# Expert tiles of 128 rows, and TensorE alternating between the next tile's first product and this tile's second

## The reference, cut to what matters

```python
x = x + xattn(layernorm(x), ctx_768, ...)             # (4, 512, 256)
n = layernorm(x)
probs = softmax(n @ Wr.T); top_v, top_i = top_k(probs, 2); top_v /= sum(top_v)
for e in range(8):
    w_e = sum(where(top_i == e, top_v, 0))
    h = gelu(n @ W1[e].T + b1[e])                     # 256 -> 1024
    out += (h @ W2[e].T + b2[e]) * w_e                # 1024 -> 256
x = x + out
```

## Time and profile before

| | before |
|---|---|
| median of 3 runs (lowest, highest) | 484.67 us (478.1, 484.67) |
| the profiled execution's own time | 480.82 us |
| its span, first to last instruction | 478.9 us |
| TensorE busy | 411.0 us, 86% |
| VectorE, ScalarE, GpSimd busy | 319.3, 198.8, 142.2 us |
| mean granted TensorE clock | 0.944 |

### The profile page before, as it was taken

The page is one execution under the profiler, slowest core; times in us unless marked ns, Lnnn a source line. Parts: engine busy times, 40 slices in busy tenths (PEclk is TensorE's granted clock), DMA queues, the critical chain, the costliest instruction groups (busy, mean ns, idle before and its releaser), DMA issues.

```text
span 478.9 us, 9857 instructions
## 1 busy us (share of the span) xinstructions
PE 411.0 (86%) x2876; PEld 317.9 (66%) x2877; DVE 319.3 (67%) x895; ACT 198.8 (42%) x339; POOL 142.2 (30%) x133
## 2 busy tenths in 40 slices
PE   3989899779898654039999999999999999999991
PEld 1345547436465543028888888888888888888880
DVE  2104755876769575917777777777777777777771
ACT  0214956775667464203443343333333434343330
POOL 8200300304253446800333222222223333222222
PEclk9999999999989975559999999999999999999997
DMA  7930037227534715240233332222222233332211
GB/s 241 327 117 0 22 117 247 90 88 237 203 121 130 258 65 167 78 144 1 46 50 67 53 53 44 46 44 44 44 44 44 44 49 62 56 54 44 44 22 23
DMA packets 32482, 43.46 MB, mean 91 GB/s; under 512 B 3088, under 2 KB 27920, under 8 KB 32336
## 3 DMA queue, kind: packets, MB, share of 16 engines
q1 hardware_dynamic: 19840, 27.24, 19.5%
q0 software_dynamic: 8880, 12.69, 13.8%
q10 hardware_dynamic: 3744, 3.31, 2.0%
HBM read 28.45 MB, written 14.78 MB: 90 GB/s over the span
## 4 chain that ended last, share of the span: by engine, by line
PE 73%; DVE 11%; ACT 4%; issue 4%; DMA 4%; POOL 2%; SPq 1%; POOLq 1%; DVEq 0%; ACTq 0%
PE o_ps L653 25%; PE s_ps L633 12%; PE t_ps L633 12%; PE proj L473 5%; PE s_ps L507 4%; PE o_ps L526 4%; PE proj L621 3%; PE proj L465 3%; DVE w2l L953 2%; PE proj L494 2%; POOL rows L404 2%; DMA xt<-rows 2%; PE proj L481 2%; PE t_ps L517 1%; DMA w2l<-ctxT 1%
## 5 line engine op out<-in xcount | busy, mean ns | idle before, releaser
L436 POOL DMA_INDIRECT out<-y,idx x46 | 72.5, 1576 | 196.7 <-DVE y L1189 189.7
L826 ACT ACTIVATE g<-s_ps,b_sb,down 128x256 f32<-128x256 f32 x92 | 46.9, 560 | 157.1 <-PE s_ps L633 157.1
L653 PE MATMUL o_ps<-w2h,gl 128*128 x368 | 100.3, 273 | 0.0
L653 PE MATMUL o_ps<-w2h,gh 128*128 x368 | 100.3, 273 | 0.0
L653 PE MATMUL o_ps<-w2l,gh 128*128 x368 | 100.3, 273 | 0.0
L1157 DVE TENSOR_SCALAR gh<-g,up 128x512 f16<-128x512 f32 x92 | 44.8, 486 | 40.9 <-ACT g L826 40.1
L1159 DVE SCALAR_TENSOR_TENSOR gl<-g,up,gh 128x512 f16<-128x512 f32 x92 | 69.1, 751 | 3.3
L826 ACT ACTIVATE g<-t_ps,b_sb,down 128x256 f32<-128x256 f32 x92 | 46.9, 559 | 13.5 <-PE t_ps L633 13.5
L404 POOL DMA_INDIRECT rows<-send,place x32 | 39.1, 1222 | 34.2 <-DVE place L1010 25.6
L653 PEld LDWEIGHTS o_ps<-w2l,gh 128*128 128x128 f16 x368 | 36.0, 98 | 4.2
L653 PEld LDWEIGHTS o_ps<-w2h,gl 128*128 128x128 f16 x368 | 36.0, 98 | 4.2
(11 more groups left out here) (160 smaller groups left out, 681.8 us busy)
## 6 DMA issues: line engine op xcount, KB each, us to landing
staged<-W1T SPq DMA_DIRECT2D x8, 1024.0 KB
staged<-W2T SPq DMA_DIRECT2D x8, 1024.0 KB
xt<-rows SPq DMA_DIRECT2D x23, 260.0 KB, 2.7
rows<-send POOLq DMA_DIRECT2D x8, 260.0 KB, 8.2
out<-x_sb ACTq DMA_DIRECT2D x4, 512.0 KB
w2l<-ctxT SPq DMA_DIRECT2D x4, 256.0 KB
x_sb<-x SPq DMA_DIRECT2D x2, 512.0 KB, 10.6
x_sb<-x ACTq DMA_DIRECT2D x2, 512.0 KB, 5.3
```

What stands on the lines that cost most here:

```text
L436: pool.indirect_dma_start(out=out, out_offset=bass.IndirectOffsetOnAxis(ap=idx[:, u, r:r + 1], axis=0), in_=y2[:, u, r, :], in_offset=None ...
L653: i = nc.tensor.matmul(y_ps[r][:, 0:D], l[:, m, r * P:(r + 1) * P], w[:, bass.ds(e, 1), m * D:(m + 1) * D].rearrange("p a n -> p (a n)"), ...
L826: i = nc.scalar.activation(g[:, m, :], h_ps[s][:, (m % MQ) * TR:(m % MQ + 1) * TR], ACT.Gelu, bias=b1_sb[:, bass.ds(e, 1), m:m + 1].rearra ...
```

## The change

The tile has 128 rows in place of 256, so `TILES` = (2·2048 + 8·127) // 128 = 39. There are 8 row buffers in place of 2. A matmul of the first product now has 128 moving columns, and there are still 48 of them to a tile; the second product has one half, so 24 matmuls with 256 moving columns. On TensorE `tile(t)` runs over the 8 chunks and at each gives out chunk `m` of the first product of tile t+1 and then chunk `m - LAG` of the second product of tile t (`LAG` = 2; the last two chunks of tile t fall into the next call). The transposes of tile t+2 stand after chunk 2. `xs`, `g`, `gh`, `gl`, `y1`, `y2` and the transposes' PSUM have two copies. The high half of the transposed rows is taken by ACT (`take_high`), the low half stays with DVE. DVE splits gelu's output in two pieces of 4 chunks each. Repeated rows get a gate of 0 (`fresh`) in place of another target, so the index arithmetic in `mark` goes, and the row number is kept as an integer. There is one scatter to a tile. The loops of PE, DVE and POOL are unrolled by 8, after 5 tiles written out (`HEAD`) and ahead of 2 (`TAIL` = 37).

```diff
-TR = 2 * P
+TR = P
-XR = 2
+XR = 8
+LAG = 2
+HEAD = 5
+TAIL = HEAD + XR * ((TILES - 2 - HEAD) // XR)
...
-                    sp.wait_ge(half_done, t * 2 - (2 * XR - 2))
+                    sp.wait_ge(added, t * 16 - (XR - 1) * 16)
...
+            def second(t, m, slot, e):
+                if m % MH == 0:
+                    pe.wait_ge(gs_ready, t * HALVES + (m // MH + 1))
+                for k, (l, w) in enumerate(((gh, w2h), (gh, w2l), (gl, w2h))):
+                    i = nc.tensor.matmul(y_ps[slot % 2][:, 0:D], l[:, slot % 2, m, :],
...
+            def tile(t, phase, ahead, e_before, e):
+                e_next = None
+                if ahead > 0:
+                    e_next = expert(t + 1)
+                    pe.wait_ge(xs_ready, t + 2)
                 for m in range(MC):
...
+                    if ahead > 0:
+                        hidden(t + 1, m, (phase + 1) % XR, e_next)
+                    if ahead > 1 and m == LAG:
+                        turn_tile(t + 2, (phase + 2) % XR)
+                    if m >= LAG:
+                        if m == LAG and (not isinstance(t, int) or t >= 2):
+                            pe.wait_ge(y_biased, t - 1)
+                        second(t, m - LAG, phase, e)
+                    elif not isinstance(t, int) or t:
+                        second(t - 1, m + MC - LAG, (phase - 1) % XR, e_before)
...
+            with pe.Fori(HEAD, TAIL - XR + 1, XR) as t:
+                experts = (expert(t - 1), expert(t))
+                for k in range(XR):
+                    experts = tile(t + k, (HEAD + k) % XR, 2, *experts)
...
+            def take_high(t, u):
+                act.wait_ge(turned, t + 1)
+                nc.scalar.activation(xs[:, u, :, 0, :], xT_ps[u][:, 0:DC * TR].rearrange("p (c n) -> p c n", c=DC),
+                                     ACT.Copy).then_inc(xs_high, 1)
```

More of the change, by code:

```diff
@@ L623, in turn_tile @@
                 i.then_inc(turned, 1)
-            def hidden(t, e):
-                pe.wait_ge(xs_ready, t + 1)
-                for m in range(MC):
[L629 to L664, removed]
+            def expert(t):
+                return pe.value_load(expert_of[0:1, bass.ds(t, 1)], min_val=0, max_val=E - 1)
+            def hidden(t, m, slot, e):
+                bank = h_ps[m // MQ]
+                if m % MQ == 0 and (not isinstance(t, int) or t):
+                    pe.wait_ge(g_ready, t * QUARTERS + (m // MQ + 1 - QUARTERS))
+                for k, (w, half) in enumerate(((w1h, 0), (w1h, 1), (w1l, 0))):
+                    for c in range(DC):
+                        at = c * M + m * P
+                        i = nc.tensor.matmul(bank[:, (m % MQ) * TR:(m % MQ + 1) * TR],
+                                             w[:, bass.ds(e, 1), at:at + P].rearrange("p a n -> p (a n)"),
+                                             xs[:, slot % 2, c, half, :], start=(k == 0 and c == 0),
+                                             stop=(k == 2 and c == DC - 1))
+                if m % MQ == MQ - 1:
+                    i.then_inc(h_full, 1)
@@ L666, in _ @@
             turn_tile(0, 0)
+            turn_tile(1, 1)
             pe.wait_ge(low_ready, UNITS)
[L668 to L673, removed]
+            experts = (None, expert(0))
+            pe.wait_ge(xs_ready, 1)
+            for m in range(MC):
+                hidden(0, m, 0, experts[1])
+            for t in range(HEAD):
+                experts = tile(t, t, 2, *experts)
@@ new lines, in _ @@
+            with pe.Fori(HEAD, TAIL - XR + 1, XR) as t:
+                experts = (expert(t - 1), expert(t))
+                for k in range(XR):
+                    experts = tile(t + k, (HEAD + k) % XR, 2, *experts)
+            experts = (expert(TAIL - 1), expert(TAIL))
+            for t in range(TAIL, TILES):
+                experts = tile(t, t % XR, min(2, TILES - 1 - t), *experts)
+            for m in range(MC - LAG, MC):
+                second(TILES - 1, m, (TILES - 1) % XR, experts[0])
@@ new lines, in tile @@
+            def tile(t, phase, ahead, e):
+                u = phase % 2
+                split(t, u, 1, e)
+                if ahead > 1:
+                    take_low(t + 2, u)
+                e_next = None
+                if ahead > 0:
+                    e_next = expert(t + 1)
+                    split(t + 1, 1 - u, 0, e_next)
+                mark(t, phase)
+                result(t, u, e)
+                return e_next
+            take_low(0, 0)
+            take_low(1, 1)
+            dve.wait_ge(b2_in, 16)
@@ L1211 @@
+            e = expert(0)
+            split(0, 0, 0, e)
+            for t in range(HEAD):
+                e = tile(t, t, 2, e)
+            with dve.Fori(HEAD, TAIL - XR + 1, XR) as t:
+                e = expert(t)
+                for k in range(XR):
+                    e = tile(t + k, (HEAD + k) % XR, 2, e)
+            e = expert(TAIL)
+            for t in range(TAIL, TILES):
+                e = tile(t, t % XR, min(2, TILES - 1 - t), e)
 def kernel(x, ctx_768, L0_xattn_Wq, L0_xattn_bq, L0_xattn_Wk, L0_xattn_bk, L0_xattn_Wv, L0_xattn_bv,
```

195 lines of the change are left out of this document (95 added, 100 removed).

## The result

The changed kernel takes 523.62 us, the median of 4 runs (522.23 to 528.71), and the kernel before 481.64 us (4 runs, 478.1 to 484.67). The ratio is 1.089, with a 95% interval of 1.077 to 1.102: 9% slower, 42 us. The profiled execution's own time is 524.5 us.

A forecast was written before the change was run, and what follows sets the result against it. The array's column streaming bounds the kernel before, TensorE's sequencer the changed one. 210.9 + 5.1 + 40.2 + 1 + 235.2 + 8 + 3.4 = 503.8, plus 9.0 and 1.9, gives 514.7; forecast 514 us, range 470 to 528.

The forecast's parts named there:

- TensorE's sequencer in place of the array: Second stage: register instructions need 0.74 us per chunk index, the array's matmuls 0.66, so the sequencer is the slower one.
- the array's pace: Rival: in timed runs the sequencer doesn't bind and the array sets 5.5 us a tile, 439.5 us; chance 0.15.
- narrow matmuls costing more: Rival: 128-column matmuls at 0.08 us; forecast stands, or 483 us with a quicker sequencer; chance 0.12 with other middling paces.
- The loop's fetch: Rival: TensorE's loop no longer fits, branches back wait 2.7 us for a fetch, 522 us; chance 0.08.
- the granted clock: Sign of being right: TensorE's clock stays at 1.00 from some 217 us on.
- Start: Second stage's start: fewer transposes and half width on DVE gain 0.9 us, first product of tile 0 at 210.9.
- Loop: TensorE's 32 loop tiles at 7.35 us are 235.2, and four round heads of 2 us are 8.
- Written-out tiles: Six tiles outside TensorE's loop at 6.7 us each, 40.2, with 1 us more while the clock is low.
- the eight row buffers: Row loads: the added buffers save nothing, since TensorE has no idle time waiting for them.
- End: Behind the loop: a written-out tile at 6.7 us, then the last tile's second product alone, 2.6 + 0.8 = 3.4 us.
- the DVE round trip: Result, then second split piece: 3.0 us against TensorE's 3.5, so no cost; 0.3 us late each tile would be 11.
- Behind the last matmul: After TensorE's last matmul: 9.0 us in place of 10.9, one scatter in the last tile saving 1.85 us.

The follow-up runs named there:

- static: Changed kernel with expert 0 for every tile on TensorE, so no reading of the expert's number or address work there; 454.47 us, ratio 0.952.
- before_static: Kernel before with expert 0 for every tile on TensorE, the choice of the expert left out; 479.03 us, ratio 1.004.
- static_w2l: Changed kernel with expert 0's weights for the `w2l` matmuls alone, 8 of 48 register instructions less a tile; 490.19 us, ratio 1.025.
- b2_third: Changed kernel with b2's load third on SP's queue, behind two row loads; 520.19 us, ratio 1.076.
- before_more: Kernel before with the expert read twice a tile, six register instructions in place of four per first-product chunk; 489.08 us, ratio 1.023.
- unrolled_pe: Changed kernel with the 32 tiles of TensorE's loop written out, nothing left out; 503.13 us, ratio 1.050.
- static_b2: Changed kernel with expert 0 for every tile on TensorE and b2's load third on SP's queue; 444.96 us, ratio 0.924.

## Why the prediction was right

The forecast was 514 us for the median and for the profiled execution 514.7; they came out at 523.6 and 524.5, so the loss is 42 us where some 34 were forecast. The mechanism, TensorE's sequencer in place of the array, is shown by static against before_static, and its price by static_w2l. The rivals (the array's pace, narrow matmuls costing more) are refuted by the same runs: the 0.055 us is there, and the array isn't what sets the pace in the change. The loop's fetch isn't a cost that shows in the change: 16 fetches of instructions, 0.26 MB, against 9, and a loop head is 2.5 to 2.6 us of idle array, which its three readings of an expert at 0.75 us and the branch account for. One sign named for being right failed: the granted clock didn't stay at 1.00 (see the last section).

By the terms of the sum:

- **Start.** First product at 211.48, predicted 210.9. The reading for tile 0's own body at 215.33, predicted 216.0.
- **Loop.** From the first head to the reading behind the last tile it is 497.23 - 255.09 = 242.1 us. Predicted were 235.2 + 8 = 243.2. Between the first and the last tile of a round the readings lie 7.18 to 7.49 us apart (predicted 7.35). That the sum is within 1.1 us is in small part luck: tiles of 7.25 us, as read above, would be 3 us less in 32, and the first tiles behind three of the heads took 7.6 to 8.2 us, with the clock at half for a part of them, which the prediction didn't have.
- **Written-out tiles.** The five ahead of the loop took 255.09 - 215.33 = 39.8 us; predicted were 5 x 6.7 + 1 = 34.5. The 5.3 us are the wait for b2 with what followed it: the gap of 4.55 us at 222.79, and after it matmuls at half the clock up to 227.2, where two wide ones are 0.21 us apart. Without the wait, in b2_third, the same five took 34.05. In the change the four tiles behind the wait took 6.75 to 7.19 us each. This term was left out: the prediction counted the eight row buffers as saving nothing, and didn't ask what SP's queue does with seven row loads ahead of b2.
- **End.** From 497.23 to the last matmul 13.9 us, predicted 6.7 + 3.4 = 10.1. Two more readings of the expert behind the loop are 1.3 us, and the clock falls behind them (below). Another 1.3 us is the DVE round trip that the prediction had weighed for each tile and found just hidden. In the loop it is, but in the last tile no first product stands between: VectorE forms tile 37's result and then splits the last piece, and TensorE waits for it at 509.88.
- **Behind the last matmul.** 522.5 - 511.08 = 11.4 us, predicted 9.0. The single scatter was to save 1.85 us, but it has to wait for the one before it to land. GpSimd's timeline, against the earlier trace rows:

```profile
509.36 1.82 POOL L437 DMA_INDIRECT out<-y,xt  x1 [3.84 <-DVE y L1223]
514.44 1.56 POOL L437 DMA_INDIRECT out<-y,xt  x1 [3.27 <-DMA out<-y,xt]
```

VectorE had the result at 512.5 us and the scatter came at 514.44. From the last matmul to the last scatter it is 3.36 us, and before it was 3.32 (471.29 - 467.97), so nothing of the 1.85 us is saved; the other 0.5 us lie behind the scatter, 8.1 us to the end of the span against 7.6.

Together -0.7 - 1.1 + 5.3 + 3.8 + 2.4 = 9.7 us, nearly all of the 9.8 between 514.7 and 524.5. The largest of them, b2's place in the queue, and the one behind the last matmul are terms that the sum had at nothing or as a gain.

Some of the prediction's figures need a word, though they move the sum little. Of the loop tile's 7.35 us both parts were off: a written-out tile takes 6.95 us and not 6.7, and the moving numbers add 0.3 and not 0.65, so the whole came out right. The 0.213 us for a wide matmul at half the clock isn't in rows 3, whose first pair gives 0.40 / 2 = 0.20. GpSimd's 4.8 us a tile doesn't follow from its terms, 1.55 + 3.9 = 5.45, and fits in 7.35 all the same. And its own cases add up to 0.19 for faster and 0.73 for slower, where it has 0.18 and 0.74.

## What to carry to other kernels

Where an address depends on a register, count the register instructions beside the matmuls: halving the width of a matmul halves the array's cover for them and leaves their number. Here four in a chunk fitted under six matmuls of 256 columns with a quarter to spare; six in a chunk used that up, and so did half the width. When a change adds buffers, look at what their first loads are queued ahead of.

## What the runs showed of the hardware

- The price of a register instruction between TensorE's matmuls is 0.11 to 0.13 us from three sides: the trace of before, where it was hidden (0.125 in the first product, 0.113 in the second), static_w2l (1.03 us for 8) and before_more (0.74 us for 6). Recorded durations of 32 to 51 ns don't show it.
- Narrow matmuls of 128 columns, each with its own full weight load, ran 0.055 us apart for a whole tile's mix in static. The Trainium skill (TensorE: Matmul & The Clock Gate, "Back-to-back issue gap") gives 81 ns sustained for such pairs; this trace doesn't agree. Its 0.055 us is near the 56 ns that the same section has for the isolated gap.
- TensorE's clock falls in the second stage once the array waits. The prediction had it at 1.00 from 217 us on. In the stretch from 220.4 to 227.1 us it is 0.51, around the gap of 4.5 us; around the loop head at 318.94 us, after a gap of 2.64 us, it is 0.67 over 4.5 us, around the first and third heads 0.69, and behind the readings at the loop's end 0.63. In these stretches wide matmuls are 0.21 us apart for a part of the time, the distance at 1.2 GHz, and 0.109 for the rest, at 2.4. Around the head at 440.0 us, with a gap of 2.60 us, the clock doesn't fall; what decides between them wasn't tried:

```profile
220.40:227.10 6.70, 4.31 (x30) 3.64 (x31) 3.62 (x7) 1.25 (x4) 0.00 (x0) 0.51 0.01 4
256.50:262.00 5.50, 4.32 (x36) 3.77 (x37) 0.84 (x2) 0.80 (x2) 0.00 (x0) 0.69 0.09 24
318.00:322.50 4.50, 3.56 (x27) 3.07 (x28) 0.56 (x2) 0.81 (x2) 0.00 (x0) 0.67 0.10 30
379.00:384.00 5.00, 4.20 (x35) 3.60 (x36) 0.84 (x2) 0.81 (x2) 0.10 (x1) 0.69 0.10 27
439.00:444.50 5.50, 4.51 (x53) 3.74 (x53) 1.41 (x4) 1.88 (x5) 0.77 (x1) 1.00 0.10 24
499.40:504.00 4.60, 4.58 (x37) 3.82 (x38) 1.23 (x3) 0.95 (x3) 0.20 (x1) 0.63 0.02 4
```

- The profiled executions with the late start (unrolled_pe, b2_third, static_b2) had a granted clock of 0.74 to 0.77 from 55 to 65 us, in the first stage, and the others 1.00 there; among the variants of the change that stage's program is the same. What makes the clock fall there was not tried and stays open.
